# Keys projected turned, pair by pair, in a decoder layer's cross attention

## What is computed

```python
def apply_rope(x, cos, sin):               # x: [b, h, s, 64], cos and sin: [512, 32]
    x1, x2 = x[..., :32], x[..., 32:]
    return concatenate([x1 * cos - x2 * sin, x2 * cos + x1 * sin], axis=-1)

lat, ctx = layer_norm(latents), layer_norm(context)
q = (lat @ Wq)                             # 16 heads of 64
k, v = split(ctx @ Wkv, 2, axis=-1)
k = apply_rope(k, cos, sin)
attn = clip(einsum('bhnd,bhsd->bhns', q, k) * 64**-0.5, -11, 11)
out = einsum('bhns,bhsd->bhnd', softmax(attn), v) @ Wo + bo
```

## Time and profile before

| | us |
|---|---|
| median of 3 runs | 442.74 (442.21 to 443.37) |
| the profiled execution | 443.53 |
| its span, first to last instruction | 441.6 |
| opening, to the first scores of round 0 | 60.65 |
| round 0 | 9.64 |
| rounds 1 to 21 | 154.75 |
| rounds 22 to 31 | 65.95 |
| expert stage | 150.61 |

### The profile page before, as it was taken

The page is one execution under the profiler, slowest core; times in us unless marked ns, Lnnn a source line. Parts: engine busy times, 40 slices in busy tenths (PEclk is TensorE's granted clock), DMA queues, the critical chain, the costliest instruction groups (busy, mean ns, idle before and its releaser), DMA issues.

```text
span 441.6 us, 8547 instructions
## 1 busy us (share of the span) xinstructions
PE 423.2 (96%) x3210; PEld 313.1 (71%) x3210; DVE 325.0 (74%) x686; ACT 195.5 (44%) x312; POOL 257.4 (58%) x225
## 2 busy tenths in 40 slices
PE   8988799999999999999999999999999999999996
PEld 8666666676667766767776666768767788888885
DVE  8998658978869767985777698797687861755554
ACT  6848364646455346362535554534437634000000
POOL 5858238998778867878769665677524850000000
PEclk9999999999999999999999999999999999999999
DMA  7766405000000000000000000435518660000000
GB/s 178 202 150 90 85 18 87 1 0 1 1 1 1 1 1 1 1 0 1 2 1 1 1 1 1 154 63 94 122 29 212 143 98 0 6 7 12 6 7 13
DMA packets 75434, 19.85 MB, mean 45 GB/s; under 512 B 66741, under 2 KB 73834, under 8 KB 75394
## 3 DMA queue, kind: packets, MB, share of 16 engines
q1 hardware_dynamic: 72628, 18.27, 19.6%
q10 hardware_dynamic: 2766, 1.04, 1.1%
HBM read 17.27 MB, written 2.02 MB: 44 GB/s over the span
## 4 chain that ended last, share of the span: by engine, by line
PE 76%; DVE 11%; ACT 5%; issue 4%; DMA 1%; ACTq 1%; POOL 1%; DVEq 0%; POOLq 0%
PE psum L1199 11%; PE psum L1182 11%; PE psum L992 9%; PE psum L1382 5%; PE psum L1383 5%; PE psum L1381 5%; PE psum L1341 4%; PE psum L1342 4%; PE psum L1343 4%; PE psum L1218 3%; PE psum L1209 3%; PE psum L1101 3%; PE psum L941 1%; ACT e_sb L806 1%; DVE rden L1607 1%
## 5 line engine op out<-in xcount | busy, mean ns | idle before, releaser
L542 POOL TENSOR_TENSOR e_part<-e_sb 128x512 f32<-128x512 f32 x64 | 89.1, 1410 | 42.1 <-DVE e_sb L1600 30.4
L806 ACT ACTIVATE e_sb<-psum 128x1024 f32<-128x1024 f32 x64 | 62.2, 1022 | 16.7 <-PE psum L1182 16.7
L1182 PE MATMUL psum<-q_t,kT 64*128 64x256 f32 x512 | 64.2, 389 | 0.0
L1199 PE MATMUL psum<-e_sb,v_sb 128*64 128x256 f32 x512 | 63.8, 386 | 0.0
L1806 DVE SCALAR_TENSOR_TENSOR x_sb<-psum,dw,x_sb 128x128 f32<-128x128 f32 x96 | 33.7, 351 | 37.4 <-PE psum L1383 34.8
L1607 DVE RECIPROCAL rden<-psum 128x256 f32<-128x256 f32 x32 | 55.8, 1745 | 0.2 <-PE psum L1209 0.2
L1600 DVE TENSOR_SCALAR e_sb<-e_sb 128x1024 f32<-128x1024 f32 x64 | 51.4, 839 | 3.8 <-ACT e_sb L806 3.8
L1182 PEld LDWEIGHTS psum<-q_t,kT 64*128 64x128 f32 x512 | 46.7, 186 | 9.6 <-issue 5.0
L785 ACT ACTIVATE kT<-psum 128x512 f32<-128x512 f32 x32 | 19.1, 598 | 77.7 <-PE psum L1101 77.3
L1199 PEld LDWEIGHTS psum<-e_sb,v_sb 128*64 128x64 f32 x512 | 33.7, 136 | 22.3 <-issue 6.6
L534 POOL TENSOR_TENSOR k_rot<-rope_a,rope_b 128x512 f32<-128x512 f32 x32 | 41.7, 1307 | 12.8 <-DVE rope_b L1487 12.8
(11 more groups left out here) (195 smaller groups left out, 780.8 us busy)
## 6 DMA issues: line engine op xcount, KB each, us to landing
w_raw<-in_L_ffn_W_dram SPq DMA_DIRECT2D x96, 64.0 KB, 2.4
gates<-gate_dram SPq DMA_DIRECT2D x6, 768.0 KB, 4.9
ctx_sb<-in_ctx_dram SPq DMA_DIRECT2D x4, 256.0 KB, 6.2
vbd<-v_dram SPq DMA_DIRECT2D x16, 52.6 KB
v_dram<-v_tok SPq DMA_DIRECT2D x4, 136.0 KB, 3.3
raw<-in_L_xattn_Wkv_dram SPq DMA_DIRECT2D x2, 256.0 KB, 4.5
k_rot<-in_L_xattn_Wkv_dram SPq DMA_DIRECT2D x2, 256.0 KB, 5.3
k_rot<-in_L_xattn_Wq_dram SPq DMA_DIRECT2D x2, 256.0 KB, 5.7
```

The lines of the kernel that those rows point to most:

```text
L542: pool.tensor_tensor(e_part[:, p % 2, half, :, :], e_sb[:, i % ERING, :, 0, :], e_sb[:, i % ERING, :, 1, :], ALU.add)\
L806: act.activation(e_sb[:, i % ERING, :, :, :].rearrange("p a k t -> p (a k t)"), psum[:, a:a + 2, :].rearrange("p a b -> p (a b)"), ACT.Exp ...
L1182: mm = pe.matmul(psum[:, 2 * (i % 2) + a, t * S:(t + 1) * S], kT[rows, p % 3, kt * P:(kt + 1) * P], q_t[rows, j % 2, p % 2, :], start=True ...
L1199: mm = pe.matmul(psum[DX * a:DX * a + DX, pv_bank(p), 0:S], v_sb[g % 2][:, kt, 2 * pp + a, :], e_sb[:, i % ERING, a, t, :], start=(kt == 0 ...
```

## The change

Keys are projected for a pair of heads and all 512 tokens of a batch: the weights' 128 columns of the pair are the stationary operand and the context (512 columns) the moving one, so the result is turned already. The number of key units stays 32, with three matmuls of 512 columns each. The rotation's tables are turned once, at the start, by 32 small matmuls into `rope_t` (cosine, signed sine); their loads move from SP's queue to ScalarE's. VectorE makes both products of a pair in one instruction of 2 x 512 (`key_products`). The halves of 32 rows of the second product must be exchanged across partitions: for the first four pairs by a matmul with a permutation (`swap_keys` on TensorE), for the others by four DMAs on SP's queue from `rope` to `raw` (`swap_keys` on SP). VectorE adds (`first_key_sum`, `key_sum`) straight into `kT`, now with four pairs. `turn_keys` on TensorE, `keys_turned` on ScalarE and `key_sum` on GpSimd are gone.

Keys have bank 6 in the rounds; values and the other work (`ASIDE`, and `LATE` where a round has two) share bank 5. On TensorE the key unit follows the value unit, then comes the aside, ahead of the weighing, which waits for the value unit's copy (`VALUES_BEFORE`). Keys run four pairs ahead (`K_LEAD`), so four key units stand in the opening and the last stands in round 27. Context turns move to rounds 1, 7 and 15. On SP the exchanges stand after the first four expert matrices and ahead of all later ones. In the opening ScalarE issues its eight shift transfers together and copies the value units later; on VectorE the product stands between the two clips, and the addition for the pair of the round before stands after the second.

The diff, cut to its core:

```diff
-    K_LEAD, V_LEAD = 2 * KC - 1, KC
+    K_LEAD, V_LEAD = 4, KC
+    KRING = 4
...
+            def swap_keys(p):                                     # SP
+                sp.wait_ge(s["rope_done"], 2 + p + 1)
+                sp.wait_ge(s["k_done"], p - 1)
+                for q in range(2 * DX // QD):
+                    to = q ^ 1
+                    sp.dma_start(raw[QD * to:QD * (to + 1), p % 2, :], rope[QD * q:QD * (q + 1), p % 2, 1, :]).then_inc(s[f"ld_raw{p % 2}"], 16)
+            for n in range(RING):
+                load_expert(n)
+            for p in range(K_LEAD, NPAIR):
+                swap_keys(p)
+            for n in range(RING, 2 * NE):
...
-                if r in ROUND_KEYS:                               # GpSimd
-                    key_sum(r + K_LEAD)
...
-            for i in range(2):                                    # ScalarE
+            for i in range(WG):
                 shift_positions(act, 1, i)
-            value_unit(4)
-            shift_positions(act, 1, 2)
             local_softmax(0)
-            value_unit(5)
-            shift_positions(act, 1, 3)
             local_softmax(1)
             weights_turned(0)
             local_softmax(2)
-            value_unit(8)
             weights_turned(1)
             weights_turned(2)
+            value_unit(4)
             local_softmax(3)
+            value_unit(5)
             local_softmax(4)
...
             for r in range(NPAIR):                                # ScalarE
                 if r + 1 < NPAIR:
                     exponent(2 * r + 2)
+                if ASIDE[r] and r in ROUND_VALUES:
+                    value_unit(ROUND_VALUES[r])
+                if r + 1 < NPAIR:
                     exponent(2 * r + 3)
...
-                if r + 3 < NPAIR:
-                    keys_turned(r + 3)
...
+                for t in range(KC):                               # TensorE, i = 0 cosine, 1 sine
+                    for q in range(2 * DX // QD):
+                        mm = turned(psum[QD * q:QD * (q + 1), 5 - i, t * P:(t + 1) * P], rope_in[:, i, t, :])
...
+            def unit_keys(m):
+                p = UNIT[m][1]
+                b, hp = divmod(p, PPB)
+                cols = slice(hp * 2 * DX, (hp + 1) * 2 * DX)
...
+                    pe.wait_ge(s["rope_done"], 2 + p)
+                pe.wait_ge(s["ctx_lo_done"], b + 1)
...
+                pe.matmul(o, wkv_hi[:, cols], ctx_hi[:, b % 2, :], start=True, stop=False)
+                pe.matmul(o, wkv_lo[:, cols], ctx_hi[:, b % 2, :], start=False, stop=False)
+                pe.matmul(o, wkv_hi[:, cols], ctx_lo[:, b % 2, :], start=False, stop=True).then_inc(s["unit_ps"], 1)
...
                 if c == 0:                                        # local_values
-                    pe.wait_ge(s["rope_done"], KC + 2)
+                    pe.wait_ge(s["v_done"], 2)
...
             for r in range(NPAIR):                                # TensorE
...
                 if r in ROUND_VALUES:
-                    route_read(2 * r - 2)
-                    unit(ROUND_VALUES[r])
-                if r % 2 == 0 and r // 2 + 1 < NQ:
-                    queries(r // 2 + 1)
+                    route_read(r - 1)
+                    unit_values(ROUND_VALUES[r])
+                if r in ROUND_KEYS:
+                    unit_keys(ROUND_KEYS[r])
+                for what in ASIDE[r]:
+                    aside(what)
+                route_1(2 * r)
                 weigh_values(2 * r)
-                route_1(2 * r)
                 weigh_values(2 * r + 1)
                 if r < NPAIR - 1:
                     sum_weights(r)
-                if r in ROUND_KEYS:
-                    route_read(2 * r)
-                    unit(ROUND_KEYS[r])
-                if r + 3 < NPAIR:
-                    turn_keys(r + 3)
+                for what in LATE[r]:
+                    aside(what)
                 route_1(2 * r + 1)
...
+            def key_products(p):                                  # VectorE
...
+                dve.tensor_tensor(rope[:, p % 2, :, :], bank(UNIT_BANK[p] if p < K_LEAD else 6)[:, None, :].to_broadcast([P, 2, SC]),
+                                  rope_t[:, :, :], ALU.mult).then_inc(s["rope_done"], 1)
+            def key_sum(p):
+                dve.wait_ge(s[f"ld_raw{p % 2}"], 16 + 16 * (2 * DX // QD) * ((p - K_LEAD) // 2 + 1))
+                dve.wait_ge(s["k_done"], p)
+                dve.wait_ge(s["score_ps"], 2 * (p - KRING + 1))
+                dve.tensor_tensor(kT[:, p % KRING, :], rope[:, p % 2, 0, :], raw[:, p % 2, :], ALU.add).then_inc(s["k_done"], 1)
...
                 if r + 1 < NPAIR:
                     clip(2 * r + 2)
+                if r in ROUND_KEYS:
+                    key_products(r + K_LEAD)
+                if r + 1 < NPAIR:
                     clip(2 * r + 3)
+                if K_LEAD <= r + K_LEAD - 1 < NPAIR:
+                    key_sum(r + K_LEAD - 1)
...
-                if r in ROUND_KEYS:
-                    key_unit(ROUND_KEYS[r])
```

More of the change, by code:

```diff
@@ L513, in _ @@
             rstd_of(LN_C, KC)
+            parts = [w[:, :].rearrange("p (a h r) -> p a h r", a=2, h=2) for w in (swap, ident)]
+            for h in range(2):
+                pool.tensor_copy(parts[0][:, :, h, :], parts[1][:, :, 1 - h, :]).then_inc(s["turn_set"], 1)
             pool.memset(bd[:, :, :], 0.0).then_inc(s["consts"], 1)
@@ L568, in _ @@
                 rstd_of(LN_C + KC * b, KC)
-            for k in range(KC, KC + 2):
-                key_sum(k)
             rstd_of(LN_C + KC * (B - 1), KC)
@@ L633, in _ @@
             act.dma_start(pos_sb[:, :], pos).then_inc(s["ld_pos"], 16)
+            for i, table in enumerate((rope_cos, rope_sin)):
+                act.dma_start(rope_in[:, i, :, :], table.rearrange("(t p) d -> p t d", p=P)).then_inc(s["ld_rope"], 16)
             act.preload_act_table(ACT.Exp)
@@ L875, in route_1, with aside @@
                     if ROUTE[stage] == i:
-                        route(0, stage, 5)
+                        route(0, stage, ROUTE_BANK.get(stage, 5))
+            def aside(what):
+                if what[0] == "context":
+                    misc_wait(what)
+                    context_f(what[1])
+                elif what[0] == "queries":
+                    queries_out(what[1])
+                elif what[0] == "latents":
+                    misc_wait(what)
+                    latents_f(what[1])
             for r in range(NPAIR):
@@ L988, in unit @@
                 o = bank(UNIT_BANK[m])
                 hi, lo = (c[:, b % 2, t * P:(t + 1) * P] for c in (ctx_hi, ctx_lo))
-                for part in parts:
-                    c, w_ = ((hi, wkv_hi), (hi, wkv_lo), (lo, wkv_hi))[part]
-                    mm = pe.matmul(o, c, w_[:, wc:wc + GC], start=(part == 0), stop=(part == 2))
-                if 2 in parts:
-                    mm.then_inc(s["unit_ps"], 1)
+                pe.matmul(o, hi, wkv_hi[:, wc:wc + GC], start=True, stop=False)
@@ L996, in relative, with swap_keys @@
+            def swap_keys(p):
+                if p == 0:
+                    pe.wait_ge(s["turn_set"], 2 * DX // QD + 2)
+                pe.wait_ge(s["rope_done"], 2 + p + 1)
+                pe.matmul(bank(UNIT_BANK[p]), swap[:, :], rope[:, p % 2, 1, :], start=True, stop=True).then_inc(s["rope_ps"], 1)
             def relative(c):
@@ L1165, in _ @@
             turn_outputs(3)
-            unit(9)
+            unit_values(7)
+            pe.wait_ge(s["v_done"], V_LEAD)
             queries(0)
@@ L1174, in scores @@
                 if half == 0:
-                    pe.wait_ge(s["misc_read"], max(MISC_NO["keys", p], MISC_NO["queries", j]) + 1)
+                    pe.wait_ge(s["misc_read"], MISC_NO["queries", j] + 1)
+                    pe.wait_ge(s["k_done"], p + 1)
                 if i >= 2:
@@ L1289, in route_1, with aside @@
                     pe.wait_ge(s["rt_done"], 2)
+                if i == ROUTE["turn"]:
+                    pe.wait_ge(s["rope_done"], 2 + NPAIR)
                 for stage in ROUTE:
                     if ROUTE[stage] == i:
-                        route(0, stage, 5)
+                        route(0, stage, ROUTE_BANK.get(stage, 5))
+            def aside(what):
+                if what[0] == "queries":
+                    queries(what[1])
+                    return
+                misc_free(what)
+                if what[0] == "context":
+                    turn_context(what[1], 5, "misc_ps")
+                elif what[0] == "latents":
+                    turn_latents(what[1], 5, "misc_ps")
+                else:
+                    project(what[1], what[2], psum[:, misc_bank(what), 0:D]).then_inc(s["misc_ps"], 1)
             for r in range(NPAIR):
@@ L1617, in add_projected @@
                 dve.wait_ge(s["misc_ps"], MISC_NO[what] + 1)
-                dve.tensor_tensor(x_sb[:, tile, :], psum[:, MISC_BANK, 0:D], x_sb[:, tile, :], ALU.add)\
```

(1 more changed line is left out.)

304 lines of the change are left out of this document (145 added, 159 removed).

## The result

The changed kernel takes 444.92 us (median of ten executions, 443.53 to 447.43) where the kernel before, on the same chip, takes 442.46 (441.73 to 443.63): a ratio of 1.0058, with an interval of 1.0041 to 1.0075. It is slower by 2.5 us. The forecast was 434.6 with a range of 429 to 442. A ratio leaves out executions more than 1.5% above the fastest of their kernel (one of six in e1, two of four in e4); a median does not.

The account below looks back on a forecast made before the run. TensorE, busy 96% of the span, was taken as the bound, with a chain of transfers and small steps in the opening. Opening +2.0, round 0 -2.9, rounds 1 to 21 -9.7 + 3.0, rounds 22 to 31 -0.5: -8.1, 434.6 us, range 429 to 442.

Parts of the forecast that it names:

- The plain round: A round on TensorE without queries: turn dropped, key unit right behind value unit, 0.64 us less, from 6.48 to 5.84.
- The new wait for the value copy: Rounds 1 to 21: TensorE work sharing bank 5 waits for ScalarE's value eviction, 0.3 us in 19 rounds.
- VectorE's lateness: Rounds 1 to 21: VectorE, 95% filled, falls behind in rounds with latent normalisations; 3.0 us taken back, bounds 0.5 and 6.
- The slack: Rounds 1 to 21: some 2.5 us between GpSimd's last additions and TensorE's need of their sum.
- The slower rival: Key addition waits for GpSimd every round, VectorE needs 7.42 us a round and decides: 445.8 us; chance 0.10.
- rounds 22 to 31, -0.5 forecast: Last rounds before the expert stage: rounds 22 to 24 gain 1.5 us, 25 to 28 lose 1.0; bounds -2.5 and +3.
- The step that failed: Rounds 25 to 27, with routing: key units add 1.95 us a round on VectorE, against 0.7 + 0.3 - 0.53 on TensorE.
- the opening, +2.0 forecast: Everything before round 0: added tables, transfers and value copies, less key turns, make it 2.0 us longer; bounds -1 and +4.
- The term for the value copies ahead of the local values: Opening: first local values wait for two value evictions with a softmax between, 1.1 us more.
- The term for VectorE: Opening: two 512-wide instructions ahead of the masks of kM; of 2 x 0.69 us about 0.5 remains after a 0.95 wait.
- the two transfers more on ScalarE: Opening: ScalarE issues all eight shift transfers before the first softmax, two more at 0.5 us each, 1.0 in all.
- no stretch gets emptier, so the clock stays out of the sum: Whole kernel: granted clock, 1.00 in all five stretches, stays as it is and gets no term.

Follow-up runs that it names:

- e1: The changed kernel with TensorE's routing step no longer waiting at the stages "chosen" and "softmax", where it has no work: 438.77 us, ratio 0.9883.
- e4: e1 with GpSimd's order in the opening turned: first two weight rests after VectorE's context normalisation, then clearing its third of the spread values; median 437.20 us.
- e11: e10 with the first product of every value and key projection of the rounds run twice on TensorE, result unchanged: 439.51 us.
- e2b: The changed kernel, wait kept, with VectorE's residual addition of round 27 ahead of the routing softmax: 441.69 us in one execution.
- e6: e1 with VectorE's residual addition of round 27 ahead of the routing softmax: 437.28 us, ratio 0.9884.
- e10: The changed kernel with the edits of e1, e6, e3 and e4 together: 433.14 us, ratio 0.9797.
- e2: The changed kernel, wait kept, with TensorE multiplying the identity into a free bank during the stop of round 27: 442.05 us in one execution.
- The repaired version: The kernel of e10, measured in two series: 433.14 us, ratio 0.9797, and 432.60 us, ratio 0.9787.
- e3: e1 with the opening's second value unit moved behind the first local values, which wait for the fourth key addition instead of its copy: 436.26 us, ratio 0.9862.

## Why the prediction was wrong

**Right: round 0 and rounds 1 to 21.** The plain round was put at 5.84 and takes 5.83, by the steps named: the turn gone and the key unit at 0.70 more. Rounds with queries were to gain 0.34 and go from 7.17 to 6.86. The new wait for the value copy was put at 0.3, and e11 shows about 0.23. Of TensorE's idle time 2.0 was to go; the four stops that it had (0.4 to 0.6 each, in rounds 6, 13, 14 and 18) are gone. Round 0 was put at 6.75 and takes 6.87.

**Wrong, to the good: VectorE's lateness.** 3.0 us were to come back in rounds 1 to 21, and the sum shows 0.4 (9.7 less 9.3). All that can be seen of it is in round 3, which takes 7.48 where it took 6.88 before: TensorE waits 0.80 there for the sums of weights, after VectorE stood for the first exchange. The products take 1217 ns and the key additions 679 at the median, 745 in the mean, where 1250 and 700 were taken; VectorE has 6.37 busy a round in place of 6.56. The durations, of products and then of key additions (ns, minimum, median, maximum):

```profile
L1526 DVE TENSOR_TENSOR rope<-psum,rope_t x32: 1191/1217/1225, 29.0 to 263.1; 128x1024 f32<-128x1024 f32 x32
```

```profile
L1541 DVE TENSOR_TENSOR kT<-rope,raw x28: 677/679/1768, 83.7 to 277.8; 128x512 f32<-128x512 f32 x28
```

The slack held; e11 shows TensorE still the bound. The slower rival, key additions blocked by GpSimd in every round, is refuted by that 679; two of the 28 took 1.43 and 1.77 us. That its 445.8 lies near the measured 444.9 is chance. The exchange lands 2.0 us after its issue, and VectorE waited for it once, 1.9 us, where 5 were taken.

**Wrong: rounds 22 to 31, -0.5 forecast, +8.3 measured.** The step that failed weighed sums of work ("three rounds of 1.95 us more on VectorE there, against 0.7 + 0.3 - 0.53 more on TensorE"). It did not go through the waits that the change adds to TensorE's routing step, one by one, though the code shows them, and the row that it rested on the earlier trace rows names the very addition that the new wait is on. TensorE's wait at "softmax" made the place of that addition in VectorE's queue the end of round 27. e1 takes 8.6 us out of rounds 26 and 27 by dropping the wait, of which 3.5 return in round 28 for the true need of bank 5; e2b takes out 3.8 by moving the addition alone. With both (e6) the stretch stands at +1.0, inside the bounds given (-2.5 and +3). A second miss hides in it: rounds 22 to 24 were to gain 1.5 and gain 0.3. In round 22 a key addition takes 1.77 us beside GpSimd, the normalisation that the routing needs comes later, and TensorE waits in round 23, which takes 8.91 (before, 8.26). So it is in nine of the eleven profiled executions with the new keys (8.73 in e11); in e2b and e4 that addition takes 0.68, and round 23 takes 7.87. No run was made for this.

**Wrong: the opening, +2.0 forecast, +6.3 measured.** The term for the value copies ahead of the local values was named but mis-sized: put at 1.1, it is 1.7 by e10 against e4. The term for VectorE counted the wait ahead of kM and took what it delayed to be covered; it did not ask what GpSimd does when the normalisation that follows comes a microsecond later. That collision cost 2.8 (e4). Without these two and at full clock the opening is at 60.45, 0.2 under before; so the other terms, which add up to +0.9, came to -0.2 together. One of them, the two transfers more on ScalarE at 0.5 each, names a row of the softmax and none of a transfer; after the change ScalarE issues its eight in 5.12 us, 0.64 each. The table turns take 1.95 us of TensorE (8.27 to 10.2), and the turned x starts 0.96 later; this was not taken away in any run, so what it costs in the end stays open.

**Wrong: "no stretch gets emptier, so the clock stays out of the sum".** Two stretches got stops of 2 to 6 us, and the clock fell behind them. In round 27 that cost 2.1 (e2). In the opening it cost up to 1.8: e1 has the same opening as the changed kernel, with the same stop of 2.82, and there the local values took 2.19, not 3.73, and round 0 started at 65.11, not 66.91. With the 2.8 and the 1.7 this makes up the 6.3, read from one execution of each kernel. How often the clock falls after such a stop is not settled; the executions of e1 went from 434.22 to 440.82.

**The sum.** The repaired version, 433.1 and 432.6, stands where the forecast stood. That does not make the forecast right: it priced the work of the change and left out the order that the change brings. The agreement is partly luck too: in the repaired kernel the opening's +2.0 and VectorE's 3.0 hardly came, and the -0.5 of the last rounds came as +1.0.

## What to carry to other kernels

When a bank or buffer gets new users, read each added wait with two questions: does the waiting engine do anything there that needs it, and where in the releasing engine's queue does the release stand? A sum of work per engine shows neither; here a wait that TensorE did not need at that place cost a round 7.8 us, and moving 0.28 us of VectorE work 2.6 us forward gave half of it back. A shift of one microsecond is worth following to the instructions that run beside it on other engines (here 2.8 us), and a stop of TensorE is to be priced with the slow products that may follow it.

## What the runs showed of the hardware that was not expected

- The same stop of TensorE, 2.82 us ahead of the local values, was followed by a granted clock of 0.53 in one execution (128 products in 3.73 us; 3.76 in e2b, 2.73 in e2) and of 1.00 in others (2.19 in e1 and in e4). Stops of 2.27, 3.01 and 5.63 us were followed by 0.68, 0.69 and 0.51; in e3 it was 0.56 from a stop of only 1.11 on.
- 28 small matmuls in a stop of 5.6 us, with gaps of 1.40 and 0.85 around them, went with a clock of 1.00 in the stop and behind it (one execution of e2).
- Four normalisations of 128x128 on VectorE took 4.07 us beside GpSimd's clearing and weight rests, and 1.10 without them; before the change, with a gap of 0.34 us between those two on GpSimd, they took 2.57. That the gap made the difference is argued from the two timelines only.
